# Two transformer layers on one core: the order of all steps as one list of 1,750 entries instead of two periodic bodies with three listed stretches

## The reference

```python
# layer 0, attention: two kinds of heads, 16 heads of 16
h = rmsnorm(x); q, k, v = h @ Wq, h @ Wk, h @ Wv
lin = causal linear attention with features [1, f, f*f] of q @ Wqf, k @ Wkf
win = softmax over the last 64 positions
x = x + ga * (h + concat(lin, win) @ Wout)
# layer 0, feed
x = x + gb * sigmoid(xr @ W_r.T) * (relu(xk @ W_k.T) ** 2 @ W_v.T)
# layer 1, attention: rotary, causal softmax, 16 heads of 16
x = x + ga * (softmax(rope(Q) @ rope(K).T) @ V @ w_proj + b)
# layer 1, feed: 256 -> 1024 -> 1024 -> 1024 -> 256, ternary weights with scales
h = silu(x @ w1) * (x @ w2); h = gelu(h @ h1); h = gelu(h @ h2); x = x + gb * (h @ w3)
```

## Time and profile before

| | |
|---|---|
| three runs | 2011.06, 2006.58, 2009.98 us; median 2009.98 |
| profiled execution | 2012.85 us, of which the span of the trace is 2011.1 |
| TensorE busy | 1871.5 us, 93% of the span |
| VectorE, ScalarE, GpSimd busy | 67%, 45%, 25% |
| mean granted TensorE clock | 0.969 of full speed |

### The profile page before, as it was taken

The page is one execution under the profiler, slowest core; times in us unless marked ns, Lnnn a source line. Parts: engine busy times, 40 slices in busy tenths (PEclk is TensorE's granted clock), DMA queues, the critical chain, the costliest instruction groups (busy, mean ns, idle before and its releaser), DMA issues.

```text
span 2011.1 us, 40494 instructions
## 1 busy us (share of the span) xinstructions
PE 1871.5 (93%) x16217; PEld 1314.3 (65%) x16217; DVE 1341.8 (67%) x2382; ACT 904.5 (45%) x1134; POOL 511.8 (25%) x597
## 2 busy tenths in 40 slices
...
DMA packets 171818, 126.36 MB, mean 63 GB/s; under 512 B 113944, under 2 KB 148720, under 8 KB 171248
## 3 DMA queue, kind: packets, MB, share of 16 engines
q1 hardware_dynamic: 170800, 123.74, 22.2%
...
## 4 chain that ended last, share of the span: by engine, by line
PE 78%; DVE 12%; ACT 6%; issue 2%; SPq 0%; DMA 0%; POOL 0%; DVEq 0%; ACTq 0%
PE ps L1999 24%; PE ps L1983 5%; PE ps L1086 4%; PE ps L1879 3%; PE ps L2013 3%; PE ps L1116 3%; PE ps L1942 3%; PE ps L991 3%; PE ps L1908 3%; PE ps L1031 3%; PE ps L1138 2%; PE ps L1922 2%; PE ps L1049 2%; PE ps L1926 2%; DVE b_maxima L1665 2%
## 5 line engine op out<-in xcount | busy, mean ns | idle before, releaser
L1999 PE MATMUL ps<-b_acts,b_hidden_w 128*128 128x512 f32 x2048 | 501.0, 397 | 0.7 <-DVEq L1741 0.7
L1999 PEld LDWEIGHTS ps<-b_acts,b_hidden_w 128*128 128x128 f32 x2048 | 376.0, 188 | 92.5 <-issue 13.6
L463 POOL TENSOR_SCALAR_AFFINE_SELECT a_probs<-a_probs 128x512 f32<-128x512 f32 (+1 forms) x224 | 167.5, 762 | 401.9 <-ACT a_probs L871 305.7
L1588 POOL TENSOR_SCALAR_AFFINE_SELECT b_work<-b_work 128x512 f32<-128x512 f32 x128 | 83.9, 667 | 670.8 <-ACT b_work L1802 670.8
L1834 ACT ACTIVATE b_acts_exact<-ps,c_s 128x512 f32<-128x512 f32 x128 | 88.2, 689 | 295.5 <-PE ps L1999 295.3
L871 ACT ACTIVATE a_probs<-ps 128x2048 f32<-128x2048 f32 (+1 forms) x96 | 153.3, 1597 | 135.1 <-DVEq L721 118.7
L1802 ACT ACTIVATE b_work<-ps 128x2048 f32<-128x2048 f32 (+1 forms) x96 | 153.3, 1597 | 100.2 <-PE ps L1926 99.9
L1665 DVE TENSOR_REDUCE b_maxima<-ps 128x4 f32<-128x2048 f32 (+3 forms) x128 | 187.9, 1489 | 3.3
L1750 DVE CAST b_acts<-b_acts_exact 128x512 fp32r<-128x512 f32 x128 | 54.8, 428 | 198.4 <-ACT b_acts_exact L1834 197.7
L1086 PE MATMUL ps<-a_probs,c_va 128*17 128x192 f32 (+4 forms) x2048 | 134.7, 383 | 2.2 <-issue 2.2
L1662 DVE TENSOR_TENSOR ps<-ps,c_causalr 128x512 f32<-128x512 f32 x128 | 86.0, 695 | 43.4 <-PE ps L1908 42.2
...
## 6 DMA issues: line engine op xcount, KB each, us to landing
b_hidden_w<-turned_h SPq DMA_DIRECT2D x128, 512.0 KB, 3.5
a_raw_next<-in_L_ffn_h_w SPq DMA_DIRECT2D x512, 16.0 KB, 1.8
...
```

What stands on the lines that cost most here:

```text
L463: return nc.gpsimd.affine_select(out=z, in_=z, compare_op=ALU.is_ge, fill=0.0, base=0, pattern=[[0, blocks_n], [1, cols]], channel_multipl ...
L1999: ins = nc.tensor.matmul(here, view(hidden_w[:, m, k]), view(src[:, k, i]), start=(k + i == 0), stop=(k == NHID - 1 and i == 1))
```

## The change

`BODY0`, `BODY1`, `START`, `TURN`, `END` and the functions that unroll and merge them go. One string `ORDER` lists all steps; `both_orders` takes it as the plan. The steps are the same 1,781; 1,471 places of the list hold another step than before. Added is one wait of DVE on its own earlier result ahead of the first maxima of each group of heads but the first.

```diff
             elif name == "wm":
                 here, free = arrive(step)
                 if step[2] == 0:
+                    if b:
+                        dve.wait_ge(shift_ready, b)
                     nc.vector.tensor_reduce(maxima[:, 0, :].unsqueeze(2), ...)
...
+ORDER = """
...
+0:pair.3 0:v.1.1 0:tk.4 0:lin.3.0 0:wt.3.1 0:lh.1 0:lv.2.0 0:again.3 0:wt.4.0 0:win.2.0 0:turn.0.0 0:wt.4.1 0:lv.2.1 0:wt.5.0 0:win.2.1 0:lv.2.2
+0:wh.1 0:wt.5.1 0:lin.3.1 0:lv.3.0 0:tk.5 0:tq.4 0:win.3.0 0:wv.2.0 0:tq.5 0:fold.4 0:wv.2.1 0:wm.4.0 0:tk.6 0:tq.6 0:lv.3.1 0:turn.0.2 0:pair.4
...
+0:wv.11.1 0:lv.12.0 0:win.12.0 0:wt.10.1 0:wh.11 0:turn.2.1 0:lv.12.1 0:turn.2.3 0:wt.11.0 0:pair.13 0:out.2.0 0:wt.11.1 0:lin.13.0 0:out.2.1
...
+0:again.23 0:lv.22.1 0:wv.22.0 0:lin.23.0 0:wt.17.1 0:qk.6.2 0:wh.21 0:wt.18.0 0:win.23.0 0:wt.18.1 0:lv.22.2 0:qk.6.3 0:lin.23.1 0:last.4.1 0:tq.24
+0:lv.23.0 0:wv.22.1 0:wt.19.0 0:tk.24 0:win.23.1 0:wh.22 0:fold.24 0:wm.24.0 0:tq.25 0:tk.25 0:wv.23.0 0:lv.23.1 0:pair.24 0:wv.23.1 0:lh.22 0:v.6.0
...
+1:proj.0.1 1:proj.0.2 1:proj.0.3 0:r.6.1 0:last.6.0 1:tk.0.0 1:tq.0.0 1:max.0.0.0 1:tk.0.1 1:tq.0.1 1:max.0.0.1 1:max.0.0.2 1:max.0.1.0 1:again.0.0
...
+1:proj.1.3 0:r.7.0 1:out.0.0 1:tk.1.0 1:tq.1.0 0:kk.7.1 1:max.1.0.0 0:r.7.1 1:max.1.0.1 1:max.1.0.2 1:out.0.1 0:last.7.0 1:again.1.0 1:att.1.0.0
...
 def both_orders():
 
-    plan = repeated(BODY0, 0) + repeated(BODY1, 1)
-    for order in ORDERS:
-        plan = in_place(plan, order)
+    plan = listed(ORDER)
```

More of the change, by code:

```diff
@@ L1208 @@
 MAX_FILLS = (((3, 0),), ((2, 0), (0, 384)), ((1, 0),))
[L1209 to L1216, removed]
@@ L1217 @@
-"""
[L1219 to L1243, removed]
@@ L1275 @@
[L1275 to L1280 removed]
+ORDER = """
+0:stats.0 0:norm.0 0:wturn.0.0 0:mod0.0 0:hT.0.0 0:hT.0.1 0:rows.0.0 0:rms.0 0:qk.0.0 0:qk.0.1 0:masks.0 0:xg.0 0:wt.0.0 0:qk.0.2 0:qk.0.3 0:wturn.0.1
@@ new lines @@
+0:again.8 0:lv.7.2 0:tk.10 0:wh.7 0:lin.8.0 0:v.2.0 0:turn.1.0 0:win.8.0 0:lh.7 0:v.2.1 0:turn.1.1 0:lin.8.1 0:wt.8.0 0:turn.1.3 0:fold.9 0:lv.8.0
+0:pair.9 0:stats.3 0:out.1.0 0:lin.9.0 0:out.1.1 0:win.8.1 0:rows.0.1 0:wv.8.0 0:xg.2 0:lv.8.1 0:lin.9.1 0:fold.10 0:tq.11 0:lv.8.2 0:wv.8.1 0:wm.10.0
+0:xT.1.0 0:again.9 0:wh.8 0:tk.11 0:pair.10 0:lv.9.0 0:lh.8 0:xT.1.1 0:win.9.0 0:again.10 0:fold.11 0:lv.9.1 0:lv.9.2 0:win.9.1 0:r.1.0 0:lin.10.0
+0:lh.9 0:kk.1.0 0:lin.10.1 0:lv.10.0 0:wv.9.0 0:wv.9.1 0:win.10.0 0:norm.3 0:kk.1.1 0:wh.9 0:wm.11.0 0:hT.3.0 0:r.1.1 0:rms.3 0:hT.3.1 0:pair.11
```

196 lines of the change are left out of this document (115 added, 81 removed).

## The result

The changed kernel takes 2047.37 us, median of 4 runs (2044.46 to 2057.91; a further execution, outside this count, took 2042.33), against 2010.52 us of before on the same chip (4 runs). The ratio is 1.0189, 95% interval 1.0151 to 1.0227: slower by 1.9% (by 1.8%, 37 us, if the two medians are compared), where 17 us were forecast, and just outside the range of 2001 to 2044. The profiled execution is the slowest run: 2057.91 us, span 2056.2. In it everything ahead of layer 1's first matmul takes 49 us longer than before.

A forecast was written before the change was run, and what follows sets the result against it. TensorE, 93% busy, was taken as the bound, its 139.6 us of idle time the stake. Terms -12 - 3 + 29 + 2 + 1 = +17 us on 2012.85 gave 2029.9, a median near 2027; range 2001 to 2044.

The forecast's parts named there:

- The reloads, +29: Layer 0's clustered wt steps: SP's queued reloads land late, DVE waits, TensorE stops; 29 us lost, 12 to 41.
- The stop at 116 us: Between wt.3.1 and wt.5.1: DVE stands still some 23 us; TensorE loses 15 and 6 us, 19 taken.
- the other two places: wt.9.0 to wt.10.0, DVE waits 2 to 3 us, 1 taken; wt.17.1 to wt.18.1, DVE waits 9, 6 taken.
- The order of SP's other work (gate rows, outputs) moves little against its users ... 0.: SP's gate rows and outputs keep nearly their distance from their users: 0 us.
- The room, -12: Fillings of the four-bank room wait less for readers: 12 us gained, most in layer 0; bounds 0 and 30.
- two signs of being wrong: DVE's reloaded-row reads show no idle time or TensorE is busy meanwhile; layer 0's regular windows lose over 15 us idle.
- the second sign: Layer 0's regular windows lose more than 15 us of idle time: the room count missed most of the gain.
- The clock, +2 (0 to 10): At the new stop after about 100 us, some 10 us of work runs at 1.2 GHz: 2 us lost.
- The passage, -3: Work put ahead of TensorE's 4.05 and 3.25 us waits for layer 1's rotated keys: 3 us gained, 0 to 5.
- Table loads, +1: ACT's Exp and Gelu changes rise from 55 to 59, at 1.28 us each: 1 us lost, 0 to 5.
- the added wait, 0: DVE waits 31 times for its own earlier result, which is long there: 0 us, at most 1.

The follow-up runs named there:

- v2: Changed kernel, clustered reloads kept, with POOL's additions on one column (work left out): 2019.41 us, ratio to before 1.0058.
- w2: Changed order with reloads spread as in x1, and POOL's additions on one column (work left out): 1988.79 us, ratio to before 0.9882.
- x1: Changed order with only its 44 wt steps moved, spreading the reloads: 2020.26 us, ratio to before 1.0037.
- x2: Changed order with eight wt steps moved later, reloads ahead of out.2 to out.4 staying: 2021.70 us, ratio to before 1.0043.
- x3: Changed order with only the eight xg steps moved later, reloads unmoved: 2042.97 us, ratio to before 1.0153.
- x4: Changed order with wt steps spread as in x1 and xg steps late as in x3: 2021.66 us, ratio to before 1.0057.
- w1: Order of before with POOL's two additions of each xg step on one column (work left out): 2004.82 us, ratio to before 0.9962.
- y3: Order of before for layer 0, changed order from layer 1's first statistics on, no added wait: 1997.47 us, ratio to before 0.9952.
- w3: Before with nothing but the added wait ahead of the first layer's maxima: 2010.20 us, ratio to before 0.9990.

## Why the prediction missed, step by step

**The terms.** Taken from the heads of single profiled executions, without additions and with spread reloads the head is 769.5 us; the changed kernel's is 826.2. Clusters alone add 27.2 (v2 less w2), additions alone 23.8 (x1 less w2), both 56.7, which leaves 5.7 for both together. Before pays 7.5 for the additions and 0 for reloads. 27.2 + (23.8 - 7.5) + 5.7 - 0.5 = 48.7, the head's whole loss. The medians of the whole time confirm the two main terms: against w2's 0.9882, clusters alone add 1.76% (35 us) and additions alone 1.55% (31 us), and before's additions cost 0.38% (8 us). They do not confirm the 5.7: both together add 3.07%, which is 5 us less than the sum. Whether the two losses strengthen each other is not shown. The executions of one such kernel differ by up to 21 us (x1: 2003.70 to 2024.92, and its profile is of the slowest).

The step that failed is a term that the prediction did not have: what POOL's additions cost DVE where the new order puts them. It is worth 16 to 24 us. Next to it the clock was taken too small, and the gain of the room did not arrive.

- *The reloads, +29.* Right in mechanism and in size: 38.4 us of DVE's waits (41 forecast), 27 us of time alone and 33 in company by the heads, 35 and 31 by the medians. The stop at 116 us came as worked out (21.1 of 23 us; TensorE's longest wait 12.0 of 15 in the first part). That the sums agree so well is partly luck. SP issues 16 transfers in 7.6 us when it doesn't pause; at `wt.11.1`, where 7 us were forecast, DVE did not wait at all; `wt.14.0` with 3.23 us was overlooked; the other two places had 3.69 (2 to 3 forecast) and 10.4 us (9). And of the 27.2 us alone only 18.2 are idle time of TensorE, the rest is its busy time (721.7 us in v2's head, 712.8 in w2's). How much of 27 is POOL's wait for gate rows stays open: v2 still had 40.6 us of it, x2's profile has a head 10 us longer than x1's, but their medians are level.
- *"The order of SP's other work (gate rows, outputs) moves little against its users ... 0."* Wrong about the waits: POOL waited for its gate row in 4 of 8 batches, 42 us in all, 13.9 at the start, where `xg.0` is moved ahead, and three times behind reloads. Only TensorE's and DVE's distances were counted. That the 0 us of time was wrong is not shown: x2, x3 and x4 find nothing clear of noise.
- *No term for POOL's additions.* The step that failed: 16 us by the heads (23.8 less before's 7.5), 22 with the part left for both together, 19 to 24 by the medians. The change part by part had no term for `xg`, which moves 3 to 7 us earlier in three batches. It priced each operation of DVE at one duration, though the earlier trace rows has 648 to 2283 ns for the same operation on L599.
- *The room, -12.* The count was right about the room and wrong about the time. Between w1 and w2 the head's waits of PE for ACT at the wide fillings (L1050, L1038, L1020 there; L1052, L1040, L1022) fall from 20.9 to 13.0 us, near the 9 that the lists gave. Waits for DVE's lower part of `fold` (L699) rise from 0.8 to 11.1. Heads 770.0 and 769.5: nothing is left. This was the prediction's own lower bound, "if other waits take the place". Neither of its two signs of being wrong came true, though it was wrong in size: DVE did wait for rows with TensorE idle, and the regular windows of layer 0 did not lose idle time, as the second sign has it, but gained 27.4 us.
- *The clock, +2 (0 to 10).* Mis-sized. "So the matmuls are fixed and the idle time is the stake" left it out: TensorE's busy time for the same 16,217 matmuls is 1871.5 us before and 1888.4 after, 16.9 us more, 9.4 of them in the head. Four other executions of the changed kernel have a mean clock of 0.957 to 0.961, the profiled one 0.951, so theirs is less by an amount that no profile shows.
- *The passage, -3.* The waits of 4.05 and 3.25 us are 2.33 and 1.95. The rest was mis-sized. Windows from L1879's first start to the projections of layer 1's third batch, in before, in the changed kernel and in y3 (columns as in the earlier trace rows):

```profile
777.00:1031.00 254.00, 200.07 (x1607) 133.52 (x1606) 170.18 (x279) 85.35 (x101) 39.15 (x46) 0.87 0.13 43
```

```profile
826.00:1077.00 251.00, 204.94 (x1606) 133.77 (x1606) 168.66 (x278) 86.41 (x102) 39.41 (x46) 0.84 0.13 43
```

```profile
778.00:1017.00 239.00, 188.94 (x1605) 124.10 (x1604) 168.69 (x278) 86.19 (x101) 39.16 (x46) 0.90 0.13 44
```

  The same 1606 matmuls take 204.9 us of TensorE in one and 188.9 in the other, with clocks of 0.84 and 0.90. The changed tail is 1216.9 to 1220.2 us in seven profiles, 1223.0 in one and 1230 in two, among them the changed kernel's; the old one is 1231.8 to 1235.2 in all six. So the order is worth about 12 to 16 us here (10 by y3's median), in y3 mostly as clock in the passage (11.1 of 15 us), and the profile after happened to show the case that gets 4. Why the passage comes out at either clock is open.
- *Table loads, +1; the added wait, 0.* 59 loads and two at the start, as counted; w3 is level.

The forecast was about +22 for the head (29 and 2, less 9 of the room) and -5 for the tail. Measured were +49 and -4 in the profiled execution, +45. If the others had a tail of -12 to -16, as most runs of this order do, +33 to +37 would come out, and the median says +37; they were not profiled. The sign was right, and for the reason given. The size missed because the head had a second loss more than half as large as the first, because the lower clock cost more than 2 us, and because the room's gain was eaten.
